# A perceiver block on one core: the 257th key's merge and the softmax division move into the cross-attention loop

## The chip, the cores and the metric

One core of one Trainium2 chip. The time is that of one execution on the device in microseconds (us); before the change it is 735.66 us, the median of 3 runs (734.97 to 736.78). The engines are TensorE (PE), VectorE (DVE), ScalarE (ACT), GpSimd (POOL) and SyncE (SP). Each runs its own instructions in program order, and they meet at semaphores. SP and ACT also issue DMAs, each from its own queue.

## What is computed

```python
x = x + xattn(layernorm(x), ctx, mask)   # 128 batches of 32 queries, 257 keys, 16 heads of 8
x = x + attn(layernorm(x))               # self-attention, 32 keys, rotary, 4 key heads
x = x + ffn(layernorm(x))                # 8 experts, one for each token
# xattn: softmax(where(mask == 0, -1e9, q k / sqrt(8))) v, times Wo, plus bo
```

The 257th key of the cross-attention is the odd one out: 256 keys fill two blocks of 128, and the last one is worked apart and merged in.

## The kernel before

**Loop.** The cross-attention takes the 128 batches in pairs: step p = 4i + r does pair p (two batches, 256 keys each), two pairs make a tile t of 128 rows of x, and 64 steps in loops over i (four steps each) make the stage. All engines go through the same steps, each with a program of its own.

**One step.** PE (`step`, L1147): the energies of pair p with the mask added (`energies`, which wait for POOL's mask `pool_m` and, once per tile, for `pool_q`), `attend` of pair p - 2, the last turn of pair p - 1, `keys` of p + 2, turn 0, `values` of p + 1, turns 1 and 2. `values` and `attend` share bank 6. DVE (L1615): three minima, `evac_out` of pair p - 2 (a copy to OC, which waits until POOL is done with that buffer, `pool_o`), the last minima, three copies of turned probabilities, the context's transpose. ACT (L665): three evacuations (`evac_k`, `evac_values`, `evac_third`), then eight exponents. POOL (`tile`, L869): for each tile the queries by head QB, two masks MZ (`masked_keys`), and `keep_own` of tile t - 3, three operations that cut the heads' own parts out of OC and put them in OT. SP (`load_pair`, L523): eight context DMAs and two mask DMAs for each pair, four pairs ahead.

**The merge.** The exponents' sums and minima of 256 keys lie in STAT. The last key's energies (`last_energies`) are taken in the last two steps of PE. After the loop, DVE takes minimum, gaps, totals and reciprocals for all tiles at once, ACT the exponents, POOL multiplies coefficients out (`coefficients`), ACT spreads them over a head's 8 columns (`spread`), PE turns them, POOL weighs the output (`weigh_out`) and forms the last key's values (`last_values`), DVE adds (`add_last`). Then PE projects (`out_project`, eight times four tiles), DVE adds the residual and takes the next layernorm's statistics. W1 is split into a high part (ACT) and a low part (POOL) at the end of that stage. Self-attention follows in a pipeline over 32 tiles, then the experts.

Of the kernel before, what the change touches and what calls it, by code (L numbers as in the profile page):

```python
# [17 lines left out]
P = 128  # L18
HD = 8
# [53 lines left out]
def perceiver_block(nc, x, ctx_in, mask, Wq, bq, Wk, bk, Wv, bv, Wo, bo,  # L73
# [18 lines left out]
    with ExitStack() as ctx:  # L92
# [55 lines left out]
        ML = sb("ML", [P, NT], I32)  # L148
        MLB = sb("MLB", [P, NT])
        VL = sb("VL", [P, P])  # L150
# [23 lines left out]

        KLT = sbc("KLT", [P, NB])
        KLB = sbc("KLB", [P, NB, 16])
        DIFF = sbc("DIFF", [P, 2, 4, NT, NG])
        MIN = sbc("MIN", [P, 4, NT, NG])
        TOTAL = sbc("TOTAL", [P, 4, NT, NG])
        COEF = sbc("COEF", [P, 2, NT, 4 * NG])  # L180
        VLT = sbc("VLT", [P, NT, P])
        OC = sbc("OC", [P, 2, BT * P])
        CX = sbc("CX", [P, 4, 2, KEYS // 32, 32])
        MK = sbc("MK", [P, 4, 2, KEYS], I32)
# [53 lines left out]
        SPREAD = TQ  # L238
        RTO = xg
        OTP = SX  # L240
        ELAST = DIFF[:, 1, :, :, :]

        CLAST = xt[:, 0, :]
        CLT = xt[:, 1, :]
        v_last = nc.dram_tensor("v_last", (NB, P), F32, kind="Internal").ap()
# [78 lines left out]
        ld_ml = sem("ld_ml")  # L324
# [7 lines left out]
        mlb_ok = sem("mlb_ok")  # L332
        st_vl = sem("st_vl")
        ld_vl = sem("ld_vl")
        pe_el = sem("pe_el")
        pe_stat = sem("pe_stat")
        m_diff = sem("m_diff")
        m_exp = sem("m_exp")
        m_inv = sem("m_inv")
        m_coef = sem("m_coef")  # L340

        act_spread = sem("act_spread")
        act_r = sem("act_r")
        pool_clv = sem("pool_clv")
        pool_t1 = sem("pool_t1")
        pe_ra = sem("pe_ra")
        pe_rb = sem("pe_rb")
        dve_otn = sem("dve_otn")
# [157 lines left out]

        small_q = [(ident, c_ident), (wv_s, Wv), (wq_s, Wq), (wo_s, Wo)]
# [9 lines left out]
        def _(sp):  # L518
# [4 lines left out]
            def load_pair(p, k, first):  # L523
# [11 lines left out]
                for e in range(2):  # L535
                    sp.dma_start(MK[:, k, e, :], mask[bass.ds(2 * p + e, 1), :, 0:KEYS]
                                 .broadcast_to([4, SQ, KEYS])).then_inc(ld_mask[k], 16)
# [3 lines left out]
            with sp.Fori(1, NP // 4) as i:  # L541
# [10 lines left out]
            sp.dma_start(ML[:, :], mask.rearrange("(i b) s k -> (b s) i k", b=BT)[:, :, KEYS],  # L552
                         allow_slow_non_contiguous=True).then_inc(ld_ml, 16)
            sp.wait_ge(st_vl, 16)
            for b in range(BT):
                sp.dma_start(VLT[b * SQ:(b + 1) * SQ, :, :],
                             v_last.rearrange("(i b a) c -> b a i c", b=BT, a=1)[b].broadcast_to([SQ, NT, P]))\
                    .then_inc(ld_vl, 16)
# [26 lines left out]
        def _(act):  # L585
# [72 lines left out]

            def evac_third(i, r):
# [22 lines left out]
            act.wait_ge(vl_ok, 1)  # L682
            act.dma_start(v_last, VL[:, :]).then_inc(st_vl, 16)
            step_range(act, step)
            evac_third(NP // 4, -1)

            act.wait_ge(m_diff, 4)
            nc.scalar.activation(DIFF[:, :, :, :, :], DIFF[:, :, :, :, :], ACT.Exp).then_inc(m_exp, 1)

            def spread(u, j):
                if u % 2 == 0:
                    act.wait_ge(m_coef, u + 1)
                wait_reuse(act, pe_ra, u - 1)
                nc.scalar.activation(SPREAD[:, j, :, :].rearrange("p i (h d) -> p (i h) d", d=HD),
                                     COEF[:, 0, 4 * u:4 * u + 4, :].rearrange("p i (h a) -> p (i h) a", a=1)
                                     .broadcast_to([P, 64, HD]), ACT.Copy).then_inc(act_spread, 1)

            def evac_inverse(u, j):
                act.wait_ge(pe_ra, u + 1)  # L700
                wait_reuse(act, pool_t1, u - 1)
                nc.scalar.activation(RTO[:, j, :], psum[6 + j][:, :], ACT.Copy).then_inc(act_r, 1)

            for u in range(NT // 4 + 1):
                if u < NT // 4:
                    spread(u, u % 2)
                if u:
                    evac_inverse(u - 1, (u - 1) % 2)

            act.wait_ge(ld_ffn, 32)
            nc.scalar.activation(W1H[:, :, :], w1_s[:, :, :], ACT.Copy).then_inc(w1_h, 1)

# [45 lines left out]
            def evac_o(t, j):  # L760
# [3 lines left out]

            act.wait_ge(n1_shift, 1)
            centre(0, 0)
            pipeline(act, [(1, evac_xv), (5, evac_probs), (-1, centre), (3, exp_scores), (5, evac_o),
                           (1, evac_last_values)], NT, 4, 6)
# [58 lines left out]
        def _(pool):  # L827
# [25 lines left out]
            def masked_keys(k):  # L853
                nc.gpsimd.tensor_scalar(MZ[:, k, :, :], MK[:, k, :, :], 0.0, None, ALU.is_equal).then_inc(pool_m, 1)  # L854
# [14 lines left out]
            def tile(i, h, first):  # L869
# [4 lines left out]
                for e in range(2):  # L874
                    masked_keys(2 * h + e)
                if not (isinstance(t, int) and t < 3):
                    keep_own(t - 3, (h + 1) % 2)

            for u in range(NT // 4):
# [6 lines left out]
                if u == 5:  # L886
                    pool.wait_ge(ld_mask[0], 32)
                    masked_keys(0)
            for k in (1, 2, 3):
                pool.wait_ge(ld_mask[k], 32)  # L890
                masked_keys(k)
                if k == 1:
                    queries_by_head(1, 1, True)
            pool.wait_ge(n0_tr, NT // 4)
# [8 lines left out]
            pool.wait_ge(klt_ok, 1)  # L903
            nc.gpsimd.tensor_tensor(
                KLB[:, :, :], KLT[:, :].rearrange("p (n a) -> p n a", a=1).broadcast_to([P, NB, 16]),
                head16[:, :].rearrange("p (a h) -> p a h", a=1).broadcast_to([P, NB, 16]), ALU.mult)\
                .then_inc(klb_ok, 1)
# [18 lines left out]
            pool.wait_ge(ld_ml, 16)  # L926
            nc.gpsimd.tensor_scalar(MLB[:, :], ML[:, :], 0.0, BIG, ALU.is_equal, ALU.mult).then_inc(mlb_ok, 1)
            for t in range(NT - 3, NT):
                keep_own(t, t % 2)

            def coefficients(c):
                cs = slice(8 * c, 8 * c + 8)
                pool.wait_ge(m_inv, c + 1)
                for w in range(2):
                    nc.gpsimd.tensor_tensor(COEF[:, w, cs, :].rearrange("p i (g k) -> p k i g", g=NG),  # L936
                                            DIFF[:, w, :, cs, :], TOTAL[:, :, cs, :], ALU.mult).then_inc(m_coef, 1)

            def last_values(u, j):
                if u % 2 == 0:  # L940
                    pool.wait_ge(m_coef, u + 2)
                wait_reuse(pool, pe_rb, u - 1)
                nc.gpsimd.tensor_tensor(SPREAD[:, 2 + j, :, :].rearrange("p i (h d) -> p (i h) d", d=HD),  # L943
# [1012 lines left out]
```

## Time and profile before

| | |
|---|---|
| median of 3 runs | 735.66 us |
| profiled execution | 738.79 us, its span 737.0 us |
| busy over the span | PE 92%, DVE 81%, ACT 68%, POOL 56% |
| mean granted clock of TensorE | 0.961 of full |

PE busy is counted from modelled ends of matmuls, so a full PE is not a PE at its peak. Idle time of an engine that does not hold the others up costs nothing. A row of a timeline begins with its start and duration in us; the square bracket at its end gives idle time of the engine before it and what ended it.

### The profile page before, as it was taken

How to read it: one execution, taken by the hardware profiler on the slowest of the kernel's cores; microseconds unless marked ns; L12 is line 12 of the kernel's file. 1: busy time of each engine (PE TensorE's matmuls, PEld its weight loads, DVE VectorE, ACT ScalarE, POOL GpSimd, SP SyncE). 2: the span in 40 equal slices, each digit the busy share in tenths (PEclk: the TensorE clock that was granted, in tenths of full speed). 3: DMA queues.
4: the chain of work that ended last, by engine and by line, in shares of the span. 5: the costliest groups of instructions: out<-in, count | busy, mean ns of one | idle time of the engine just before them, and what ended most of it. 6: DMA issues, size and time to landing. Idle time of an engine off the chain costs nothing.

```text
span 737.0 us, 29352 instructions
## 1 busy us (share of the span) xinstructions
PE 678.4 (92%) x9915; PEld 529.0 (72%) x9915; DVE 595.0 (81%) x1460; ACT 501.9 (68%) x1561; POOL 414.7 (56%) x435
## 2 busy tenths in 40 slices
PE   4999999999999999999999955999999849999994
PEld 2577777777777777777777744787777638888894
DVE  6688888888888888888888768488888857779484
ACT  3788888888888888888888634355555445545552
POOL 4576536546464564645455287467777648207375
PEclk9999999999999999999999989599999959999998
DMA  8444444444444444444448082000000020003721
GB/s 179 93 89 89 89 86 87 96 92 92 88 89 92 94 91 89 86 91 92 90 89 134 12 256 53 2 4 5 1 0 2 3 72 1 1 1 108 227 80 42
DMA packets 186527, 55.06 MB, mean 75 GB/s; under 512 B 146708, under 2 KB 184856, under 8 KB 186466
## 3 DMA queue, kind: packets, MB, share of 16 engines
q1 hardware_dynamic: 182768, 49.74, 31.8%
q0 software_dynamic: 1824, 3.96, 1.6%
q8 instruction: 40, 0.66, 0.4%
q10 hardware_dynamic: 1874, 0.54, 0.4%
q14 instruction: 21, 0.17, 0.1%
HBM read 44.51 MB, written 8.83 MB: 72 GB/s over the span
## 4 chain that ended last, share of the span: by engine, by line
PE 85%; DVE 7%; POOL 3%; issue 2%; ACT 1%; DMA 1%; POOLq 0%; ACTq 0%; DVEq 0%
PE bank L502 39%; PE energy L502 23%; PE bank L505 23%; POOL SX L951 1%; POOL TQ L943 1%; DVE stats L1534 1%; DMA X<-in_x 1%; PE energy L505 1%; DVE STAT L1592 0%; POOL COEF L936 0%; POOL out L1034 0%; DVE xn L1517 0%; DVE stats L1696 0%; DVE SX L1737 0%; DVE smx L1732 0%
## 5 line engine op out<-in xcount | busy, mean ns | idle before, releaser
L653 ACT ACTIVATE PR<-energy,STAT 128x256 f32<-128x256 f32 x512 | 235.6, 476 | 50.3 <-DVE STAT L1586 49.9
L505 PE MATMUL bank<-ident,PR 128*128 128x128 f32 x1024 | 160.2, 282 | 0.8 <-DVE PT L1612 0.8
L505 PEld LDWEIGHTS bank<-ident,PR 128*128 128x128 f32 x1024 | 112.5, 141 | 62.9 <-issue 33.6
L1612 DVE COPY PT<-bank 128x512 f32<-128x512 f32 x192 | 126.1, 684 | 11.4 <-PE bank L505 10.6
L847 POOL TENSOR_TENSOR QB<-QT,headmask 128x512 f32<-128x512 f32 x32 | 33.3, 1042 | 157.5 <-DMA MK<-in_mask_BxSxS_ik 99.1
L653 ACT ACTIVATION_READ_ACCUMULATOR PR<-energy,STAT (+1 forms) x512 | 105.5, 206 | 0.0
L854 POOL TENSOR_SCALAR MZ<-MK 128x512 bf16<-128x512 int32 x64 | 94.3, 1489 | 8.3 <-DMA MK<-in_mask_BxSxS_ik 8.3
L1592 DVE TENSOR_REDUCE STAT<-energy 128x512 f32 (+1 forms) x128 | 87.3, 682 | 0.0
L1586 DVE TENSOR_REDUCE STAT<-energy 128x256 f32 (+1 forms) x128 | 48.4, 420 | 39.3 <-PE energy L502 39.3
L502 PE MATMUL bank<-PT,VT 128*32 128x128 f32 x2048 | 69.2, 276 | 0.1
L502 PE MATMUL bank<-wv_s,CT 128*128 128x128 f32 x512 | 67.8, 275 | 0.5 <-issue 0.5
L502 PEld LDWEIGHTS bank<-PT,VT 128*32 128x32 f32 x2048 | 52.0, 109 | 21.4 <-issue 19.1
L502 PE MATMUL energy<-KS,QB 32*128 32x256 f32 x1024 | 66.1, 374 | 0.0
L502 PE MATMUL bank<-CT,wk_s 128*128 128x512 f32 x128 | 65.6, 594 | 0.0
L502 PEld LDWEIGHTS bank<-wv_s,CT 128*128 128x128 f32 x512 | 62.4, 192 | 1.0 <-issue 1.0
L752 ACT ACTIVATE SX<-SX 128x512 f32<-128x512 f32 x32 | 20.2, 631 | 52.6 <-DVE SX L1737 52.6
L502 PEld LDWEIGHTS energy<-KS,QB 32*128 32x128 f32 x1024 | 49.6, 185 | 3.5
L502 PE MATMUL energy<-w_s,TQ 128*128 128x128 f32 x384 | 48.1, 277 | 1.1 <-ACT TQ L793 0.9
L502 PEld LDWEIGHTS energy<-w_s,TQ 128*128 128x128 f32 x384 | 45.7, 192 | 3.8 <-ACT TQ L793 1.9
L987 POOL TENSOR_TENSOR SX<-SX,sinv 128x512 f32<-128x512 f32 x32 | 33.6, 1049 | 26.4 <-DVE sinv L1747 26.4
L1556 DVE STREAM_TRANSPOSE CT<-CX 128x512 f32<-128x512 f32 x64 | 44.9, 702 | 1.5 <-DMA CX<-in_ctx 1.5
L621 ACT ACTIVATE KS<-bank,bias 128x512 f32<-128x512 f32 x64 | 45.3, 709 | 0.6 <-PE bank L502 0.6
(272 smaller groups left out, 1410.2 us busy)
## 6 DMA issues: line engine op xcount, KB each, us to landing
CX<-in_ctx SPq DMA_DIRECT2D x512, 32.0 KB, 2.5
MK<-in_mask_BxSxS_ik SPq DMA_DIRECT2D x128, 128.0 KB
rows_in<-fill SPq DMA_DIRECT2D x1, 3483.0 KB, 19.6
X<-in_x SPq DMA_DIRECT2D x4, 512.0 KB, 7.4
VLT<-v_last SPq DMA_DIRECT2D x4, 512.0 KB, 9.9
PAY<-rows_in SPq DMA_DIRECT2D x2, 903.0 KB, 7.4
PAY<-X SPq DMA_DIRECT2D x1, 1280.0 KB, 6.8
w_s<-in_L_ffn_W SPq DMA_DIRECT2D x1, 1024.0 KB, 5.4
```

The source lines that it names most:

```text
L502: return nc.tensor.matmul(o, l, r, start=start, stop=stop, skip_group_check=True)
L505: return nc.tensor.transpose(o, i, ident[0:n, 0:n])
L621: nc.scalar.activation(KS[:, k % 2, :], psum[0][:, :], ACT.Identity, bias=bias[:, 1:2])\
L653: nc.scalar.activation(PR[:, b, g, :], EB[:, g, e * KEYS:(e + 1) * KEYS], ACT.Exp, bias=STAT[:, bass.ds(t, 1), b, 1, g:g + 1].rearrange("p ...
L752: nc.scalar.activation(SX[:, j, :, :], SX[:, j, :, :], ACT.Exp, scale=SCALE).then_inc(a_ex, 1)
L847: nc.gpsimd.tensor_tensor(QB[:, k, :, :, :], QT[:, bass.ds(t * P, P)].rearrange("p (b a q) -> p b a q", b=BT, a=1).broadcast_to([P, BT, 4, ...
L854: nc.gpsimd.tensor_scalar(MZ[:, k, :, :], MK[:, k, :, :], 0.0, None, ALU.is_equal).then_inc(pool_m, 1)
L987: nc.gpsimd.tensor_tensor(SX[:, j, :, :], SX[:, j, :, :], sinv[:, j, :].rearrange("p (n a) -> p n a", a=1).broadcast_to([P, 16, SQ]), ALU. ...
L1556: V.transpose(CT[:, k % 2, :], CX[:, k, :, :, :].rearrange("p e n i -> p (e n i)")).then_inc(ev_l, 1)
L1586: V.tensor_reduce(STAT[:, bass.ds(t, 1), 2 * (k % 2), 1, g:g + 1].rearrange("p a g -> p (a g)"), EB[:, g, 0:KEYS], AX_X, ALU.min).then_inc ...
L1592: V.tensor_reduce(STAT[:, bass.ds(t, 1), b:b + 2, 1, g:g + 1].rearrange("p a b g -> p (a b g)"), EB[:, g, :].rearrange("p (e k) -> p e k", ...
L1612: V.tensor_copy(PT[:, k % 2, u, :, :], psum[1 if u % 2 else 7].rearrange("p (n k) -> p n k", n=2))\
```

## The change

The 257th key's energies are taken in steps 0 and 1 (PE), turned in step 2, and kept. The division and the merge are made per group v of two tiles (four pairs) in the loop. DVE: `last_energy` in step (v, 3), `gaps`, `totals`, `coefficients` in steps 0 to 2 of iteration v + 1, each in up to three parts between and behind its copies, the last a transpose to COEFT. ACT: `gap_exponents` in step 1 of iteration v + 1; in iteration v + 2 it stores COEFT to DRAM in step 0 (`send_coefficients`), and in steps 2 and 3 it loads the third and fourth quarter back, each row to the 8 columns of its head (`spread_coefficients`, 64 KB each). SP loads the first two quarters between its pair loads. POOL weighs the output of group i - 2 at the end of its iteration i, with three operations on 256 columns, and notes the last key's mask in `masked_keys`. The two late query blocks both go to step 0. What stood in the merge stage goes, but for the two last groups; the projection reads OT. W1's split goes in eight pieces into the self-attention pipeline (`weights_high`, `weights_low`, steps 4 to 11).

```diff
@@ def send_coefficients / spread_coefficients (new; eng is SP or ACT)
+        def send_coefficients(eng, v):
+            eng.wait_ge(m_turned, v + 1)
+            eng.dma_start(coef_rows[bass.ds(v, 1), :, :].rearrange("a p c -> p (a c)"), COEFT[:, :]).then_inc(st_cf, 16)
+
+        def spread_coefficients(eng, v, groups):
+            eng.wait_ge(st_cf, 16 * v + 16)
+            tail = static(v) and v == NV - 1
+            if not tail:
+                wait_reuse(eng, pool_t1, v)
+            for g in groups:
+                eng.dma_start((COEFL if tail else COEFS)[32 * g:32 * g + 32, :, :, :].rearrange("p n w q -> p (n w q)"),
+                              coef_rows[bass.ds(v, 1), :, :].rearrange("a (h g n) c -> g h a (n c)", h=4, g=NG)[g]
+                              .broadcast_to([4, HD, 16 * SQ])).then_inc(ld_cl if tail else ld_cf, 16)
@@ SP (the mask loads take all S2 = 257 keys)
+            with sp.Fori(3, NP // 4) as i:
+                for k in range(4):
+                    load_pair(i * 4 + k, k, False)
+                    if k == 1:
+                        spread_coefficients(sp, i - 3, (0, 1))
+            spread_coefficients(sp, NV - 3, (0, 1))
...
+            for v in (NV - 2, NV - 1):
+                send_coefficients(sp, v)
+                spread_coefficients(sp, v, range(NG) if v < NV - 1 else (0, 1))
+            sp.wait_ge(ld_cl, 16 * NG)
@@ ScalarE, step(i, r), between evac_third(i, r - 1) and the exponents
+                if r == 1 and not (start and p < 4):
+                    gap_exponents(i - 1)
+                elif not (start and p < 8):
+                    if r == 0:
+                        send_coefficients(act, i - 2)
+                    else:
+                        spread_coefficients(act, i - 2, (r,))
@@ GpSimd
-            def masked_keys(k):
-                nc.gpsimd.tensor_scalar(MZ[:, k, :, :], MK[:, k, :, :], 0.0, None, ALU.is_equal).then_inc(pool_m, 1)
+            def masked_keys(p, k):
+                nc.gpsimd.tensor_scalar(FL[:, k, :], MK[:, k, :, KEYS], 0.0, None, ALU.is_equal).then_inc(pool_f, 1)
+                nc.gpsimd.tensor_scalar(MZ[:, k, :, :], MK[:, k, :, 0:KEYS], 0.0, None, ALU.is_equal)\
+                    .then_inc(pool_m, 1)
+                pool.wait_ge(pool_f, 2 * p + 1)
+                nc.gpsimd.tensor_copy(MLS[:, bass.ds(2 * p, 2)], FL[:, k, :]).then_inc(pool_f, 1)
+            def weigh_out(v):
+                if static(v) and v == NV - 1:
+                    pool.wait_ge(ld_cl, 16 * NG)
+                else:
+                    pool.wait_ge(ld_cf, 16 * NG * v + 16 * NG)
+                pool.wait_ge(pool_o, 2 * v + 2)
...
+                nc.gpsimd.tensor_tensor(out_t(2 * P * v), out_t(2 * P * v), coef[:, :, 0, :], ALU.mult).then_inc(pool_w, 1)
+                nc.gpsimd.tensor_tensor(coef[:, :, 1, :], coef[:, :, 1, :],
+                                        VLD[:, bass.ds(8 * v, 8)].rearrange("p (n a) -> p n a", a=1)
+                                        .broadcast_to([P, 8, SQ]), ALU.mult).then_inc(pool_w, 1)
+                pool.wait_ge(pool_w, 2 * v + 2)
+                nc.gpsimd.tensor_tensor(out_t(P * (2 * v + 1) - P), out_t(P * (2 * v + 1) - P), coef[:, :, 1, :], ALU.add).then_inc(pool_t1, 1)
...
             with pool.Fori(2, NT // 2) as i:
                 for k in range(2):
                     tile(i, k, False)
+                weigh_out(i - 2)
...
+            keep_own(NT - 3, (NT - 3) % 2)
+            weigh_out(NV - 2)
+            keep_own(NT - 2, (NT - 2) % 2)
+            keep_own(NT - 1, (NT - 1) % 2)
+            weigh_out(NV - 1)
@@ TensorE
+                if start and p == 0:
+                    pe.wait_ge(ev_w, 1)
+                    pe.wait_ge(n0_xt, NT // 4)
+                    queries(LATE_Q, 0)
+                    queries(LATE_Q + 1, 1)
+                elif start and p == 1:
+                    last_energies(1)
                 else:
                     attend(i, r - 2)
+                if start and p == 2:
+                    turn_energies()
...
                 if now:
                     turn(i, r, 0)
+                if start and p == 0:
+                    last_energies(0)
                 if not (start and p + 1 >= NP):
                     values(i, r + 1)
...
             def out_project(u, j):
-                pe.wait_ge(dve_otn, u + 1)
+                pe.wait_ge(pool_t1, 2 * u + 2)
...
+            pe.wait_ge(act_exp, 4 * NB)
+            out_project(0, 0)
+            step(NP // 4, 1)
+            for u in range(1, NT // 4):
+                out_project(u, u % 2)
@@ VectorE
+            def merge(i, r, part):
+                if r == 3:
+                    if part == 0:
+                        last_energy(i)
+                elif not (static(i) and i == 0):
+                    (gaps, totals, coefficients)[r](i - 1, part)
...
                     evac_turned(i, r, 0)
+                    if start and p == 0:
+                        evac_energies(slice(0, 64 * LATE_Q), 1)
+                    merge(i, r, 0)
                     evac_turned(i, r, 1)
+                    merge(i, r, 1)
                 if not (start and p + 3 >= NP):
                     turn_context(i, r + 3)
+                if not last:
+                    merge(i, r, 2)
...
-            for u in range(NT // 4 + 1):
-                if u < NT // 4:
-                    add_last(u, u % 2)
...
+            for u in range(NT // 4):
+                cross_residual(u, u % 2)
+                cross_statistics(u)
```

## Rows read from the trace of the kernel before

**Rows 1.** Busy by stretch: start:end, length; PE, PEld, DVE, ACT, POOL; PEclk, DMA, GB/s.
```profile
200.00:400.00 200.00, 200.00 (x2558) 149.46 (x2551) 175.65 (x328) 173.56 (x621) 106.89 (x116) 1.00 0.47 92
...
430.00:440.00 10.00, 7.79 (x48) 6.72 (x48) 4.61 (x10) 4.11 (x8) 9.84 (x13) 0.78 1.08 315
...
462.00:472.00 10.00, 9.50 (x129) 7.93 (x128) 3.00 (x7) 2.16 (x5) 3.53 (x4) 0.50 0.01 2
...
490.00:580.00 90.00, 88.04 (x2752) 69.67 (x2752) 78.56 (x195) 48.54 (x120) 67.31 (x74) 1.00 0.01 2
```

**Rows 2.** Timeline around one step of the loop (energies to energies).
```profile
201.47 1.04 POOL L847 TENSOR_TENSOR QB<-QT,headmask 128x512 f32<-128x512 f32 x1 [4.78 <-DMA MK<-in_mask_BxSxS_ik]
...
202.48 2.94 POOL L854 TENSOR_SCALAR MZ<-MK 128x512 bf16<-128x512 int32 x2
...
205.39 1.04 POOL L860 TENSOR_TENSOR OC<-OC,headmask 128x512 f32<-128x512 f32 x1
...
205.54 0.40 PE L502 MATMUL energy<-MZ,SEL_Q 32*128 32x512 bf16 x4
...
206.50 0.73 POOL L864 TENSOR_TENSOR OC<-OC 128x256 f32<-128x256 f32 x1
...
206.94 0.76 DVE L1586 TENSOR_REDUCE STAT<-energy 128x256 f32 x2 [0.58 <-PE energy L502]
...
207.42 0.46 POOL L866 TENSOR_TENSOR OT<-OC 128x128 f32 x1 [0.18 <-POOL OC L864]
...
208.21 0.41 DVE L1607 COPY OC<-bank 128x256 f32<-128x256 f32 x1
...
210.75 0.48 ACT L653 ACTIVATE PR<-energy,STAT 128x256 f32<-128x256 f32 x1
...
211.66 0.40 PE L502 MATMUL energy<-MZ,SEL_Q 32*128 32x512 bf16 x4
```

**Rows 3.** Timeline, last steps of the loop and what follows.
```profile
407.72 0.39 PE L502 MATMUL energy<-MZ,SEL_Q 32*128 32x512 bf16 x4
...
414.69 0.40 PE L502 MATMUL energy<-MZ,SEL_Q 32*128 32x512 bf16 x4
...
425.59 0.42 DVE L1607 COPY OC<-bank 128x256 f32<-128x256 f32 x1
```

**Rows 4.** Timeline, end of the merge stage.
```profile
453.00 4.52 POOL L966 TENSOR_TENSOR W1L<-w_s,W1H 128x2048 fp32r<-128x2048 f32 x1 [0.53 <-ACT W1H L712]
...
454.62 0.67 DVE L1691 TENSOR_TENSOR X<-X,energy 128x512 f32<-128x512 f32 x1
...
455.33 0.87 DVE L1696 BATCH_NORM_STATS2 stats<-X 128x6 f32<-128x128 f32 x4
...
457.64 0.20 DVE L1499 TENSOR_TENSOR std<-stats 128x32 f32<-128x32 f32 x1
```

**Rows 5.** Instructions of line 683, the store of v_last from ACT's queue.
```profile
DMA to landing us min/median/max: 3.8/3.8/3.8
```

**Rows 6.** Timeline, start of the loop.
```profile
27.95 0.39 PE L502 MATMUL energy<-MZ,SEL_Q 32*128 32x512 bf16 x4
...
28.06 0.37 ACTq L683 DMA_DIRECT2D v_last<-VL  x1
...
29.26 0.66 ACT L621 ACTIVATE KS<-bank,bias 128x512 f32<-128x512 f32 x1
...
31.44 1.06 PE L502 MATMUL bank<-wv_s,CT 128*128 128x128 f32 x8
...
31.76 0.68 DVE L1598 TENSOR_REDUCE STAT<-energy 128x2 f32<-128x512 f32 x1
```

**Rows 7.** Costliest groups: copies of turned probabilities; xcount, busy us, mean ns.
```profile
L1612 DVE COPY PT<-bank 128x512 f32<-128x512 f32 x192 | 126.1, 684 | 11.4 <-PE bank L505 10.6
```

**Rows 8.** Instructions of tile CX, the context loads of 32 KB.
```profile
DMA to landing us min/median/max: 1.6/2.5/3.8
```

**Rows 9.** Timeline of SP's queue in the loop.
```profile
195.09 1.31 SPq L536 DMA_DIRECT2D MK<-in_mask_BxSxS_ik  x2
```

More of the change, by code:

```diff
@@ L680, in _ @@
             evac_k(0, 1)
-            act.wait_ge(vl_ok, 1)
-            act.dma_start(v_last, VL[:, :]).then_inc(st_vl, 16)
             step_range(act, step)
             evac_third(NP // 4, -1)
[L687 to L702, printed above, removed]
-            for u in range(NT // 4 + 1):
-                if u < NT // 4:
[L706 to L712, printed above, removed]
+            gap_exponents(NV - 1)
+            spread_coefficients(act, NV - 1, (2, 3))
             act.wait_ge(lg_tr, 1)
@@ L763, in evac_o, with weights_high @@
                 nc.scalar.activation(SO[:, j, :], psum[7][:, 0:P], ACT.Copy).then_inc(a_so, 1)
+            def weights_high(t, j):
+                if static(t) and 4 <= t < 4 + E:
+                    if t == 4:
+                        act.wait_ge(ld_ffn, 32)
+                    nc.scalar.activation(W1H[:, t - 4, :], w1_s[:, t - 4, :], ACT.Copy).then_inc(w1_h, 1)
             act.wait_ge(n1_shift, 1)
@@ new lines, in totals @@
+            def totals(v, part):
+                if part == 0:
+                    dve.wait_ge(m_exp, v + 1)
+                    V.tensor_tensor(by_group(SUM[:, :]), by_group(GAP[:, 0, :]), own_stats(v, 0), ALU.mult)\
+                        .then_inc(m_own, 1)
+                elif part == 1:
+                    dve.wait_ge(m_own, 6 * v + 3)
+                    V.tensor_tensor(SUM[:, :], SUM[:, :], GAP[:, 1, :], ALU.add).then_inc(m_own, 1)
+                else:
+                    dve.wait_ge(m_own, 6 * v + 4)
+                    V.reciprocal(SUM[:, :], SUM[:, :]).then_inc(m_own, 1)
@@ new lines, in coefficients @@
+            def coefficients(v, part):
+                if part == 0:
+                    dve.wait_ge(m_own, 6 * v + 5)
+                    V.tensor_tensor(COEF[:, :, :], GAP[:, :, :],
+                                    SUM[:, :].rearrange("p (a n) -> p a n", a=1).broadcast_to([P, 2, 8 * NG]),
+                                    ALU.mult).then_inc(m_own, 1)
+                elif part == 2:
+                    dve.wait_ge(m_own, 6 * v + 6)
+                    wait_reuse(dve, st_cf, 16 * v)
+                    V.transpose(COEFT[:, :], COEF[:, :, :].rearrange("p w n -> p (w n)")).then_inc(m_turned, 1)
@@ L1622, in step @@
                     pair_minimum(i, r, 2)
-                if start and p < 2:
-                    evac_query(LATE_Q + p)
-                else:
+                if start and p == 0:
+                    evac_query(LATE_Q)
+                elif not (start and p < 2):
                     evac_out(i, r - 2)
+                if start and p == NP:
+                    for part in range(3):
+                        totals(NV - 1, part)
+                    for part in range(3):
+                        coefficients(NV - 1, part)
                 if not last:
@@ L1629, in step @@
                     second_minimum(i, r)
+                if start and p == 0:
+                    evac_query(LATE_Q + 1)
+                if start and p == 1:
+                    evac_energies(slice(64 * LATE_Q, 16 * NT), 2)
+                if start and p == 2:
+                    dve.wait_ge(pe_el, 3)
+                    V.tensor_copy(ELS[:, :, :].rearrange("p g (t b) -> p b t g", b=BT),
+                                  psum[7].rearrange("p (b t g) -> p b t g", b=BT, g=NG)).then_inc(el_ok, 1)
                 if not (start and p < 1):
```

277 lines of the change are left out of this document (103 added, 174 removed).

## Prediction

> **What bounds the kernel now.** I read the chain of waits first: it runs through TensorE, step after step, until the merge stage, and there from engine to engine. Then the busy times by stretch. Between 200 and 400 us PE is busy all 200 us, DVE 175.7, ACT 173.6, POOL 106.9 [rows 1]. So the loop is held by PE, and POOL, whose work nearly all moves are made to, looks half free. Then the timeline of one step. A step lasts 6.12 us (energies at 205.54 and 211.66) [rows 2]. DVE sat idle 0.58 us before its first minimum, and the last exponent (210.75, 0.48 and a read of some 0.2) is done about 0.25 us before the next energies: small slacks. POOL waits 4.78 us for a mask before it starts a tile [rows 2]. What is to be seen there is not the idle time but the order: POOL is one queue, and each tile's masks must pass through it before PE may begin that pair's energies. Last the stage behind the loop: energies of pair 63 at 414.69 [rows 3], last statistics ended at 456.20 (455.33 + 0.87) [rows 4], 41.5 us.
>
> **What goes: the merge stage.** In the new order, out_project(0) to (6) need no coefficient later than group 13, so DVE's residuals may follow right behind evac_out(63). Before, that copy ends at 426.01, 11.3 us after the energies of pair 63 [rows 3]. Eight times a residual (0.67) and four statistics (0.87) [rows 4] are 12.3 us, so statistics end 23.6 us after those energies, not 41.5: 17.9 less. Late next is the coefficient chain of group 15: coefficients at about +9 (DVE's three gap, three total and two coefficient operations lie between its copies), sent with 3.8 us [rows 5], spread with another 3 to 4, weigh_out 2.4, projection 1.2, residual and statistics 1.5: about 22. The two ends are close, so 14 to 18 may go; I take 17.8. Pair 62 also loses last_energies: its step took 6.97 us (407.72 to 414.69) [rows 3], 0.9 over a plain one. I take 0.9; zero is the other end, if that step is long for another reason. TensorE's granted clock was 0.50 (1.2 of 2.4 GHz) in 462 to 472 [rows 1], after the idle end of the merge. An idle end stays, so I leave that as it is; if it goes, up to 5 us more are saved in that stretch.
>
> **What is added at the start.** In step 0 values(1) waits until DVE has emptied bank 6 of the last energies. DVE's second minimum ends at 32.44 (31.76 + 0.68) [rows 6]; behind it now come the second query copy, a turned copy and the energies' copy, about 0.69 each by the 128x512 copies [rows 7] and the last smaller: 34.3. values(1) began at 31.44 [rows 6]; 2.9 later, less some 0.3 of small waits that it swallows: 2.6. Step 1: a short copy, 0.2. In step 2 the first turn waits for the 512-column copy that follows the second minimum, so it ends 4.49 (31.76 + 0.68 - 27.95) + 0.69 = 5.2 us into the step; with the turn's 0.6 behind it, values come at 5.8 where they came at 3.5 (31.44 - 27.95) [rows 6]: 2.3, less 0.5. Together 4.6; 3 to 6 as bounds. The widened key product KLB moves from a gap of POOL to one, and I cost it at nothing: what hides it is that POOL then waits for the third mask anyway; uncovered it is 1 us.
>
> **What is added in the loop, small operations.** Per four steps DVE gets nine operations on 32 or 64 columns. The nearest row has 0.20 us for 32 columns [rows 4], and they follow each other faster than that. That is at most 0.6 us in a step, as much as the 0.58 idle [rows 2]. I take 1 us over the whole loop. If the cover is gone (the full 0.2 and a wait for each, 0.4 us over the idle time per four steps), it is 6.6. ACT's gap exponents lie in the wait for the first minimum. The DMA instructions on ACT cost it nothing: the store of v_last was issued at 28.06 while an evacuation that stands ahead of it in the program began at 29.26 [rows 6], so the queue's front runs ahead of the engine. SP issues two spreads and waits for a store once per four pairs; as masks then come earlier than POOL wants them, I cost it at nothing, 1 us if its lead is used up.
>
> **What is added in the loop, the wait on POOL.** This decides. In iteration i POOL does tile(i, 0), tile(i, 1), weigh_out(i - 2). weigh_out needs all four spreads of that group, and ACT issues the fourth only in its step 4i + 3. Queued behind it on POOL is tile(i + 1, 0), whose masks PE needs for step 4i + 4, just one step later. Time counts from the energies of step 4i + 3:
> - ACT issues at +0.15: the copy ahead of it waits for the last turn of the step before, which ends there. If the queue did not run ahead it would be +1.2.
> - Landing. The trace has no such transfer. The context's 32 KB land in 1.6, 2.5 and 3.8 us (least, median, most) [rows 8]; v_last's 64 KB from ACT's queue took 3.8 [rows 5]. For masks (128 KB), the pair issued at 195.09 is what I take POOL to have got at 201.47 [rows 2, 9]; the second, issued halfway through the 1.31 us, took 5.7. I take 3.15, the mean of 2.5 and 3.8, since the spread is 64 KB on ACT's queue but is loaded like the context. 1.6 and 5.7 are kept for the range.
> - weigh_out: three operations on 256 columns at 0.73, with 0.18 before the dependent one, as in keep_own [rows 2]: 2.37.
> - QB 1.01 (201.47 to 202.48), the mask's new flag some 0.2 (0.46 for 128 columns bounds it), one mask 1.47 (half of 2.94) [rows 2], and 0.1 twice for semaphores.
>
> The sum is 0.15 + 3.15 + 2.37 + 1.01 + 0.2 + 1.47 + 0.2 = 8.55, against 6.12: PE stands 2.4 us.
>
> A second wait follows in the same step. DVE's evac_out needs keep_own(2i - 1), which stands in tile(i + 1, 0) behind both masks: 0.6 of small operations, 1.47, and keep_own's 2.49 (205.39 to 207.88) [rows 2] make it ready 4.45 us after the energies, where DVE wants it at 2.67 (208.21 - 205.54) [rows 2]. Queued behind evac_out on DVE are the last two minima, behind those the last four exponents, behind those the next energies. 1.78 less the 0.25 of slack is 1.5 us. Before, POOL ran more than a step ahead and neither wait was there.
>
> It happens where a further tile follows in the loop: i = 2 to 14, 13 times. 13 x (2.4 + 1.5) = 50.7.
>
> The Trainium skill (DMA: Bandwidth & Descriptors, section "Why a DMA increments its semaphore by 16 and not by 1") says that a transfer runs on as many of the 16 DMA engines, at most, as divide the slowest dimension of both its sides. By that the spread, with 4 on its source side, would run on 4 engines, and so would the mask, whose source is 4 copies; the mask's landing would be the nearer row. No row here shows how many engines a transfer had. The sum would then be the second rival's below.
>
> **The sum.** 4.6 + 1 + 50.7 - 17.8 - 0.9 = +37.6. The profiled execution took 738.79 (span 737.0 and 1.79 around it), 3.1 above the runs' median of 735.66; the difference carries over, so 735.66 + 37.6 = 773.
>
> **W1's two halves** move into the self-attention loop, eight pieces on ACT and POOL. POOL is busy 67.3 of 90 us there [rows 1], and the whole subtraction took 4.52 [rows 4], 0.57 a piece in steps of some 3.6. I cost that at nothing; 0 to 2 us if it delays the rotation queued behind it.
>
> **The rivals.**
> - *The wait on POOL does not bind, and the kernel is faster.* If POOL got the coefficients before it wants them, only start, small operations and tail would be left: 735.66 + 4.6 + 1 - 18.7 = 722.6. It decides at a landing of 0.7 us or less for the first wait (8.55 - 3.15 = 5.4 of fixed work in 6.12), and the least landing of the context is 1.6 [rows 8]. Halfway: landing 1.6 costs 0.9 each time, 11.7, and if DVE's late copy is also made up somewhere, the time is 734. For it speaks POOL's half-free share and its 4.78 us of waiting; against it that this idle time lies ahead of tiles whose masks were not needed yet, and that the order of the queue is fixed. 14 in 100, 3 of them halfway.
> - *The spread lands like a mask.* 5.7 instead of 3.15 makes the first wait 5.0: 13 x 6.5 = 84.5, together +71.4, 807. PE would then stand long enough for its clock to matter. Between 430 and 440 the granted clock was 0.78 after the idle front of the merge [rows 1], that is 4.4 us at half clock and 2.2 lost; 13 times 29 more, 836. For it speaks that masks are loading at that moment on the same engines; against it that a spread is half a mask, and not two at once. 15 in 100.
> - *SP is the one that is late.* It waits for the store of group i - 3 before it loads the next pairs. Per four pairs it issues for about 23 us of 24.5; with 5 us of waiting it would be 4 to 5 late. But PE is slower by 3.9 too, and the masks lead by a tile. If it does bind on top of the forecast by 1 us each time, 786. 6 in 100.
>
> **How the numbers follow.** The forecast, POOL's order stopping PE by 3 to 5 us in each iteration, has 65 in 100 and by itself 757 to 790 (landing 1.9 to 4.4). The range 750 to 806 leaves out most of the faster rival and the upper part of the mask-like one. Faster by over 0.3% (what a measurement of this kernel can tell, 2.2 us): 11 in 100. Within: 3, the halfway case. Slower: 86.
>
> **What would show it.** Right: idle time of PE before the energies of every fourth step, put down to POOL's masks (about 30 us in total); POOL waiting before weigh_out for the spread from ACT's line; DVE waiting for POOL before every fourth OC copy; four steps together 28 us in place of 24.5; the stage behind the last energies some 18 us shorter. Wrong: POOL's weigh_out starting without a wait, or steps that stay at 6.12 throughout. The size is wrong if the landing is under 1.9 or over 4.4 us.

## The result and the profile after

The changed kernel takes 810.96 us (median of 4 runs, 808.82 to 815.58) where the one before took 736.22 (median of the 4 runs beside it): ratio 1.1024, 95% interval 1.0967 to 1.108. The forecast was 773, with a range up to 806. The direction was right, the size was not.

The profiled execution has a span of 813.8 us, 76.8 over the one before. The starts of the energies divide that sum. From step 0 to step 3 it takes 8.1 us more, from step 3 to 11 nothing, from step 11 to 63 86.8 more, and from step 63 to the end 18.0 less (and 0.1 less ahead of step 0). The forecast had +4.6 for the start, +50.8 for the loop (its terms less 0.9) and -17.8 for the end. So the error is nearly all in the loop.

Windows of the kernel after (columns as in [rows 1]): the 200 us of the loop shown before, three pieces around one stop of PE, and two in the stage behind the merge.
```profile
200.00:400.00 200.00, 166.72 (x1951) 123.61 (x1950) 144.79 (x305) 135.20 (x482) 101.71 (x152) 0.91 0.36 75
...
206.00:207.00 1.00, 0.00 (x0) 0.00 (x0) 0.00 (x0) 0.00 (x0) 1.00 (x2) 1.00 0.00 0
207.00:208.00 1.00, 0.30 (x4) 0.31 (x8) 0.00 (x0) 0.00 (x0) 1.00 (x4) 0.81 0.00 0
208.00:211.00 3.00, 3.00 (x40) 2.12 (x40) 0.81 (x3) 0.15 (x1) 2.92 (x4) 0.50 0.15 42
...
543.00:548.00 5.00, 4.50 (x62) 3.70 (x63) 1.05 (x3) 0.77 (x2) 1.76 (x2) 0.50 0.99 297
548.00:553.00 5.00, 4.67 (x150) 3.75 (x145) 4.01 (x10) 2.04 (x5) 3.00 (x4) 0.90 0.03 9
```
PE was busy all 200 us before [rows 1]; now 33 of them are gone. POOL is busy for half of them, as it was (101.7 against 106.9): it is not short of time, its wait stands in the wrong place. The waits of the kernel after (engine, line, what it waited for: us, times, longest) say where:
```profile
POOL OT L898 <- DMA COEFS<-coef_rows: 209.4, 15, 15.9
...
PE energy L498 <- POOL MZ L858: 58.3, 13, 5.5
...
DVE OC L1595 <- POOL OT L873: 5.9, 6, 3.2
```
PE waits for POOL's mask 13 times, as forecast, but for 58 us, not 30. DVE's copy, forecast to wait for POOL each time too, does so five times in the loop, for 2.6 us together; the sixth, of 3.2, lies behind the loop. One of the 13 iterations, the timeline of the step that [rows 2] showed before:
```profile
196.01 1.31 SPq L547 DMA_DIRECT2D MK<-in_mask_BxSxS_ik  x2
...
196.83 0.40 PE L498 MATMUL energy<-MZ,SEL_Q 32*128 32x512 bf16 x4
...
197.13 0.63 ACTq L515 DMA_DIRECT2D COEFS<-coef_rows  x1
...
202.69 0.72 POOL L898 TENSOR_TENSOR OT<-OT,COEFS 128x256 f32 x1 [14.63 <-DMA COEFS<-coef_rows]
...
204.20 0.72 POOL L903 TENSOR_TENSOR OT<-OT,COEFS 128x256 f32 x1 [0.21 <-POOL COEFS L899]
204.88 1.04 POOL L850 TENSOR_TENSOR QB<-QT,headmask 128x512 f32<-128x512 f32 x1
...
206.07 1.49 POOL L858 TENSOR_SCALAR MZ<-MK 128x512 bf16<-128x512 int32 x1
...
207.70 0.62 PE L498 MATMUL energy<-MZ,SEL_Q 32*128 32x512 bf16 x4 [4.68 <-POOL MZ L858]
...
211.94 0.42 DVE L1595 COPY OC<-bank 128x256 f32<-128x256 f32 x1 [0.39 <-POOL OT L873]
```
Read it from the energies at 196.83, as the forecast's sum does. ACT issues at +0.30, the spread is there at +5.86, so it took 5.56 where 3.15 stood; weigh_out takes 2.19, QB 1.01, flag and mask 1.67, and the energies come 0.14 later, at +10.87. The chain is the forecast's, link by link; the landing alone is off. Over the 13 iterations the landing is 5.36 us (4.43 to 6.36), and the steps from 4i + 3 on last 10.67, 8.09, 6.35 and 6.14 us, against 6.13 before. The excess over four plain steps is 6.73 an iteration, 87.5 in all, where the sum had 3.9 and 50.7. The second step's excess (1.96) is larger than the forecast's second wait (1.5), and the clock goes with the difference. After its stop PE ran at a granted clock of 0.50, that is 1.2 of 2.4 GHz (windows above). In four of the 13 iterations, the one shown among them, the clock was back at 1.00 after 3.4 us, and the second step lasts 7.69 to 7.70, which is the forecast's; in the other nine it stayed at 0.50 for 6.8 us, and the second step lasts 7.80 to 8.59.

### The profile page after: what moved, and what is told of

Read it like the earlier page. It is cut to its first block, busy times and chain, and to the rows that moved or that the text cites. A ratio compares the mean times of both kernels' runs of the same rounds, so it can differ in the third digit from the quotient of the medians.

```text
span 813.8 us, 30118 instructions
## 1 busy us (share of the span) xinstructions
PE 698.5 (86%) x9851; PEld 540.8 (66%) x9851; DVE 611.1 (75%) x1577; ACT 497.2 (61%) x1567; POOL 443.9 (55%) x593
## 4 chain that ended last, share of the span: by engine, by line
PE 56%; POOL 11%; DVE 9%; DMA 9%; ACT 6%; issue 6%; POOLq 1%; DVEq 1%; ACTq 0%
PE bank L498 24%; PE energy L498 20%; PE bank L501 12%; DMA COEFS<-coef_rows 8%; ACT PR L667 4%; POOL MZ L858 2%; POOL QB L850 2%; POOL OT L898 1%; DVE STAT L1574 1%; POOL COEFS L899 1%; POOL SX L979 1%; POOL KB L971 1%; DVE PT L1600 1%; DVE stats L1522 1%; ACT KS L635 1%
## 5 line engine op out<-in xcount | busy, mean ns | idle before, releaser
L501 PE MATMUL bank<-ident,PR 128*128 128x128 f32 x1024 | 162.1, 287 | 3.8 <-DVE PT L1600 3.7
L501 PEld LDWEIGHTS bank<-ident,PR 128*128 128x128 f32 x1024 | 115.7, 143 | 67.8 <-issue 34.4
L898 POOL TENSOR_TENSOR OT<-OT,COEFS 128x256 f32 (+1 forms) x15 | 10.9, 727 | 209.4 <-DMA COEFS<-coef_rows 209.4
L858 POOL TENSOR_SCALAR MZ<-MK 128x512 bf16<-128x512 int32 x64 | 96.0, 1500 | 0.0
L498 PE MATMUL bank<-PT,VT 128*32 128x128 f32 x2048 | 80.0, 304 | 4.3 <-DVE PT L1600 4.3
L498 PEld LDWEIGHTS bank<-PT,VT 128*32 128x32 f32 x2048 | 59.5, 121 | 30.6 <-issue 24.5
L498 PE MATMUL energy<-MZ,SEL_Q 32*128 32x512 bf16 x256 | 27.9, 425 | 58.3 <-POOL MZ L858 58.3
L498 PE MATMUL energy<-KS,QB 32*128 32x256 f32 x1024 | 77.4, 425 | 0.0
L498 PEld LDWEIGHTS energy<-KS,QB 32*128 32x128 f32 x1024 | 57.1, 211 | 5.1
L498 PEld LDWEIGHTS energy<-MZ,SEL_Q 32*128 32x128 bf16 x256 | 6.6, 92 | 70.5 <-issue 66.8
```

What stands on the lines that cost most here:

```text
L498: return nc.tensor.matmul(o, l, r, start=start, stop=stop, skip_group_check=True)
L501: return nc.tensor.transpose(o, i, ident[0:n, 0:n])
L858: nc.gpsimd.tensor_scalar(MZ[:, k, :, :], MK[:, k, :, 0:KEYS], 0.0, None, ALU.is_equal)\
L898: nc.gpsimd.tensor_tensor(out_t(2 * P * v), out_t(2 * P * v), coef[:, :, 0, :], ALU.mult).then_inc(pool_w, 1)
```

## The experiments

**The late spread removed, four ways.** Theory T: the fourth spread's landing and the order on POOL's queue make the loss. Each of four kernels breaks one link of it.

ACT loads both its quarters in step 2:
```diff
-                    else:
-                        spread_coefficients(act, i - 2, (r,))
+                    elif r == 2:
+                        spread_coefficients(act, i - 2, (2, 3))
```

> ACT loads both its quarters in step 2, the fourth one step earlier. Theory T (the fourth spread's late landing stops POOL, whose queue holds the masks, 6.6 us in each of 13 iterations, 85 us in all): the first wait goes, a part of the second (DVE's evac_out behind keep_own) stays at about 0.9 us each time: 811 - 85 + 12 = 738. Rival S (the small operations and issues added to DVE and ACT cost it, not the landing): 805 to 811. Rival C (the spreads' traffic holds up masks and context on the DMA engines): above 770.

Measured: 741.58 us (738.12 to 748.95), 1.0051 of before (1.0014 to 1.0088). The first wait shrinks to 0.22 (step 6.35), the next step is 7.27, 1.14 over. T holds, within 4 us.

The same, but in step 1, behind `gap_exponents`:
```diff
                 if r == 1 and not (start and p < 4):
                     gap_exponents(i - 1)
...
+                    if not (start and p < 8):
+                        spread_coefficients(act, i - 2, (2, 3))
...
```

> ACT loads both its quarters in step 1, the fourth two steps earlier. T: both waits gone, 811 - 85 = 726, with steps of 6.13 us throughout. Rival S: 805 to 811. Rival C: above 770. If only the second wait mattered beside the first, the step from the run with step 2 to this one is worth about 12 us.

Measured: 739.90 (736.43 to 744.04), ratio 1.0027 (0.9998 to 1.0056), 14 us over the 726 expected. Both waits are gone (steps 6.12 and 6.15), but step 1 now lasts 6.99. Its timeline shows a cost that the forecast had put at nothing:
```profile
197.60 0.74 DVE L1573 TENSOR_REDUCE STAT<-energy 128x256 f32 x2
197.70 0.26 ACT L676 ACTIVATE GAP<-GAP 128x64 f32<-128x64 f32 x1 [0.33 <-DVE GAP L1633]
...
197.97 1.48 ACTq L515 DMA_DIRECT2D COEFS<-coef_rows  x2
...
199.69 0.47 ACT L667 ACTIVATE PR<-energy,STAT 128x256 f32<-128x256 f32 x1 [1.73 <-DVE STAT L1579]
...
200.76 0.44 PE L501 MATMUL bank<-ident,PR 128*128 128x128 f32 x2 [0.93 <-ACT PR L667]
```
The exponent at 199.69 is put down to one of DVE's minima (L1579), but it needs only the two before (L1573), and these ended at 198.34. What ended at 199.45 is ACT's own issuing. ACT's queue did not run ahead of the engine here: the gap exponents ahead of the two issues waited until 197.70, so the issues, 0.74 each, stood between them and the exponents, and PE waited 0.93.

SP loads all four quarters:
```diff
                     if k == 1:
-                        spread_coefficients(sp, i - 3, (0, 1))
+                        spread_coefficients(sp, i - 3, range(NG))
...
@@ ScalarE
-                    else:
-                        spread_coefficients(act, i - 2, (r,))
```

> SP loads all four quarters in step 1 or 2, ACT none. T: 726 as long as SP keeps up. The rival that SP is late: two more issues of some 0.65 us on 23 us in 24.5 and the wait for the store make it fall behind, masks come late: 740 to 786. S: 805 to 811 unless ACT's issues are what costs.

Measured: 754.56 (752.40 to 756.90), ratio 1.0202 (1.0150 to 1.0254). The rival's case: SP is late. Four steps take 27.00 us, and in that kernel SP's spreads follow each other after 26.8, with no long pause in its queue. Its lateness comes in by the same door: POOL waits for the spread ahead of weigh_out again, PE for the mask behind it (12 times, 9.5 us), and DVE's copy for keep_own (13 times, 19.1 us).

POOL weighs one tile later, transfers unchanged:
```diff
-            with pool.Fori(2, NT // 2) as i:
-                for k in range(2):
-                    tile(i, k, False)
-                weigh_out(i - 2)
+            with pool.Fori(3, NT // 2) as i:   # iteration 2 is peeled, group 13 follows
+                tile(i, 0, False)
+                weigh_out(i - 3)
+                tile(i, 1, False)
```

> The transfers stay as they are; POOL weighs group i - 3 between the two tiles of iteration i, so that no mask stands behind a fresh spread. T: 726, for the order on POOL is what makes the landing cost. C (traffic): stays above 770. S: 805 to 811.

Measured: 736.17 (733.71 to 740.64), ratio 0.9989 (0.9959 to 1.0019). With the same DMAs in flight and the same small operations on DVE and ACT, the order on POOL alone gives 75 us back; rivals S and C can't explain these. That is the cause shown. But it is 10 us over the 726 expected: four steps take 25.31. SP's queue in this kernel:
```profile
198.59 1.51 SPq L515 DMA_DIRECT2D COEFS<-coef_rows  x2
200.39 3.84 SPq L541 DMA_DIRECT2D CX<-in_ctx  x8
204.41 1.36 SPq L547 DMA_DIRECT2D MK<-in_mask_BxSxS_ik  x2
...
222.13 1.33 SPq L547 DMA_DIRECT2D MK<-in_mask_BxSxS_ik  x2
223.80 1.51 SPq L515 DMA_DIRECT2D COEFS<-coef_rows  x2
```
From spread to spread 25.21 us, issuing nearly without a pause. So SP holds the loop here: masks come late, keep_own after them, and DVE's copy waits for it (11.4 us, 13 times). SP has no long pause in the two kernels with ACT's early loads either (spread to spread 25.1 to 26.1 us). So what the second wait and ACT's issuing cost them stands beside a bound of SP that is nearly as long, and no run here takes the two apart.

**What the landing is made of.** Three kernels hold back only a part of the fourth quarter until step 3, the rest goes in step 2; here with two heads late:
```diff
+        CUT = [(2, 4, 0, 8), (0, 2, 0, 8)]   # heads, pairs of rows: early, late
...
+                    elif r == 2:
+                        spread_coefficients(act, i - 2, (2, 3), 0)
                     else:
-                        spread_coefficients(act, i - 2, (r,))
+                        spread_coefficients(act, i - 2, (3,), 1)
```

> The fourth quarter in two halves, two heads of four each (32 KB, 2 rows on the source's slowest side): one half in step 2, the other late in step 3. If the landing follows the bytes, half of what lies over the store's 1.5 us goes: 1.5 + 4.06 / 2 = 3.5 us from issue to weigh_out, and the first wait falls by 2 us, time some 811 - 27 = 784 or, as PE's clock then keeps up, 775. If it follows the count on the slowest side (2 here, 4 in the whole quarter), the late half takes as long as the whole: 5.5 us and 811.

> The same with the other cut: half of each row, all four heads (32 KB, 4 rows on the source's slowest side). Bytes and slowest side both say 3.5 us from issue to weigh_out; the time is then that of the forecast's own landing of 3.15, 773 plus what the start costs more (3.4): about 775 to 784. If landing is a fixed latency or the wait for other traffic: 5 us or more and 805 to 811.

> One head of four is late (16 KB, slowest side 8 for what is copied 8 times). By bytes 1.5 + 4.06 / 4 = 2.5 us from issue to weigh_out; by the slowest side (8 in place of 4, a quarter of the bytes) 2.0. A fixed latency: 5 us. Time by T at 2.5 us: first wait 1.7 us and the second 1.5, 13 x 3.2 = 42 where after had 85: about 765.

And two kernels leave the spread whole and thin SP's loads, so that they compute something else:
```diff
-                        sp.dma_start(CX[rows, k, e, :, :], ctx_in[..., 0:KEYS, rows] ...
+                        sp.dma_start(CX[rows, k, e, 0:KEYS // 32 if first else 2, :], ctx_in[..., 0:KEYS if first else 64, rows] ...
```

> Changed computation: from pair 4 on only 64 of 256 context rows of a batch are loaded, by as many DMAs as before; the rest of CX is old. Theory Q (the spread's landing, 5.3 us on the mean of 13, is its quiet 3.1 us and 2.2 us of queueing behind SP's loads on the DMA engines): with three quarters of the context's packets gone it falls to between 3.1 and 4 if the context is what it waits behind, and each iteration's loss falls by 2 us or more: 811 - 26 = 785 or less. Rival M (it waits behind the masks): 5 us and 805 to 811. Rival L (a fixed latency of what follows a store or runs on ACT's queue): 5.3 us.

```diff
-                    sp.dma_start(MK[:, k, e, :], mask[..., :] ...
+                    sp.dma_start(MK[:, k, e, 0:cols], mask[..., 0:cols] ...   # cols = S2 if first else 64
```

> Changed computation: from pair 4 on only 64 of 257 mask columns are loaded (256 B in place of 1028 B a row), by as many DMAs. Theory Q with the masks as what it waits behind: 3.1 to 4 us of landing and 785 or less. Rival (the context is what it waits behind): 5 us and 805 to 811. If each has a share, both runs land between 4 and 5.

Measured, one execution of each but the first; the landings are means over iterations 2 to 14 (least to most), taken from the timelines of ACT's queue, SP's queue and POOL; the last column is group 13, whose spread has no mask or context load beside it:

| kernel | time us | from the late issue to weigh_out | from the mask pair's issue ahead of it | group 13 |
|---|---|---|---|---|
| after | 810.96 | 5.36 (4.43 to 6.36) | 7.05 (6.28 to 7.46) | 3.09 |
| two heads late, 32 KB | 814.06 | 5.39 (4.74 to 6.47) | 6.80 (5.75 to 7.55) | 2.72 |
| half rows late, 32 KB | 808.48 | 5.10 (4.30 to 6.02) | 6.39 (4.92 to 7.00) | 2.45 |
| one head late, 16 KB | 808.41 | 5.06 (4.32 to 5.81) | 6.56 (5.04 to 7.53) | 2.41 |
| quarter of the context | 802.84 | 4.48 (3.73 to 5.45) | 6.65 (6.47 to 7.14) | 3.01 |
| quarter of the masks | 780.97 | 3.18 (2.90 to 3.59) | 4.50 (4.02 to 6.93) | 3.01 |

For the smaller pieces the landing that follows the bytes missed in all three: a quarter of the bytes lands 0.3 us sooner. What came is each text's other case, in which the bytes do not count (about 5 us or more). The piece's size and its cut hardly matter, for it waits behind the mask pair. The fourth column shows it best in the run with little context: spreads issued 1.1 us after the masks took 5.4, those issued 2.8 after took 3.9, and both were there 6.5 to 6.9 after the masks. That run met neither of its two numbers, and of the context's own share it leaves little: counted from the masks, the landing falls by 0.4. With thin masks the landing is 3.18, about that of a quiet queue. So a spread of 64 KB costs 3.1 us by itself, and the other 2.2 are the masks ahead of it, though these are on SP's queue and it is on ACT's. The Trainium skill (DMA: Bandwidth & Descriptors, section "Issuing engines are not separate DMA queues") says that transfers run on the same 16 DMA engines and interleave, whichever engine started them; these runs agree that the engines are the same.

The prediction found no row on how many of the engines a transfer had. The traces hold the packets, and these show it. In the kernel before, only masks moved between 196.3 and 198; there the share of the 16 engines (the last number but one) is 0.23, that is 3.7 engines. In the kernel after, in the step shown above, ACT's queue (q10) has no packet between its issue at 197.13 and 200.8 (first line), while the masks move; then the whole spread passes within 1 us, on 23.2% of 16, again 3.7 engines (the next two lines):
```profile
196.30:198.00 1.70, 1.70 (x13) 1.32 (x12) 1.70 (x4) 1.70 (x8) 0.39 (x1) 1.00 0.23 68
...
q1 hardware_dynamic: 950, 0.34, 37.2%
...
q1 hardware_dynamic: 538, 0.07, 43.0%
q10 hardware_dynamic: 34, 0.07, 23.2%
```
```profile
DMA packets 37, 0.07 MB, mean 61 GB/s; under 512 B 4, under 2 KB 4, under 8 KB 36
...
DMA packets 18, 0.03 MB, mean 27 GB/s; under 512 B 2, under 2 KB 2, under 8 KB 18
...
DMA packets 36, 0.03 MB, mean 27 GB/s; under 512 B 4, under 2 KB 36, under 8 KB 36
...
DMA packets 16, 0.02 MB, mean 14 GB/s; under 512 B 8, under 2 KB 8, under 8 KB 16
```
These are the counts on the source's slowest side (4 heads, 2 heads, 4 heads, and the 8 copies of the one head), by which the rule that the prediction cited counts the engines; the trace agrees with it. So mask and spread each had four engines, and as the spread stood still until the masks were all but through, these must have been the same four. The piece of one head, with eight, shows it within one transfer: issued at 195.67 behind a mask pair, half of its 16 packets pass between 197.2 and 197.7, none in the next 1 us, and the other half between 198.7 and 199.0, just after the last packet of the masks (198.5):
```profile
q10 hardware_dynamic: 8, 0.01, 4.7%
...
q10 hardware_dynamic: 8, 0.01, 7.8%
```
Half of it was not held up, but weigh_out needs all of it.

The run with thin masks is the forecast's own case, measured. Its timeline:
```profile
190.21 0.39 PE L498 MATMUL energy<-MZ,SEL_Q 32*128 32x512 bf16 x4
...
190.50 0.63 ACTq L515 DMA_DIRECT2D COEFS<-coef_rows  x1
...
193.70 0.73 POOL L899 TENSOR_TENSOR OT<-OT,COEFS 128x256 f32 x1 [12.22 <-DMA COEFS<-coef_rows]
...
198.73 0.40 PE L498 MATMUL energy<-MZ,SEL_Q 32*128 32x512 bf16 x4 [2.34 <-POOL MZ L859]
...
202.97 0.42 DVE L1596 COPY OC<-bank 128x256 f32<-128x256 f32 x1 [1.46 <-POOL OT L874]
```
PE stands 2.34 us and DVE's copy 1.46, where 2.4 and 1.5 were forecast; the steps are 8.50 and 7.71. It takes 780.97. Its start alone is 4.8 us dearer than forecast; without these it is 3 us over the 773.

**SP relieved too.** POOL's own queue loads all four quarters, one iteration later; it had over 4 us of waiting per tile [rows 2]. SP and ACT load none in the loop, and the last two groups stay as they were:
```diff
+                spread_coefficients(pool, i - 3, range(NG))
                 for k in range(2):
                     tile(i, k, False)
-                weigh_out(i - 2)
+                weigh_out(i - 3)
...
```

> POOL's own queue loads all four quarters of group i - 3 ahead of tile(i, 0) and POOL weighs that group behind tile(i, 1); SP and ACT load none in the loop. Theory SP (with POOL's order mended, what is left of the loop's loss is SP's issue time: 25.2 us in four steps with two spreads in the run with POOL's order changed, 26.7 with four): steps of 6.13 us throughout, loop 368 us, time 736 - 9 = 727. Rival (ACT's issue, or DVE's small operations cost that): 733 to 740. Rival (POOL is long in issuing, over 4 us for four): masks come late, over 740.

Measured: 730.57 (728.02 to 733.84), ratio 0.9932 (0.9911 to 0.9953), 0.7% faster than before. Steps are 6.15, 6.14, 6.13 and 6.15. Its loop window and the issuing on POOL:
```profile
200.00:400.00 200.00, 199.75 (x2551) 148.85 (x2544) 189.01 (x402) 174.47 (x625) 148.79 (x225) 1.00 0.50 101
```
```profile
220.36 2.63 POOL L516 DMA_DIRECT2D COEFS<-coef_rows  x4 [0.84 <-POOL OT L902]
```
PE is full again. Four issues cost POOL 2.63 us in four steps, inside its waits. DVE carries the merge at 189 busy us of 200 without holding PE up, so the small operations cost nothing that shows.

**The start.** In step 0 of the kernel after, PE stops inside the burst of last-key matmuls, and nothing in the profile is waited for:
```profile
32.23 1.17 PE L498 MATMUL bank<-KLB,QT 128*32 128x16 f32 x117
35.26 1.04 PE L498 MATMUL bank<-KLB,QT 128*32 128x16 f32 x75 [1.86 <-issue]
37.03 2.05 PE L498 MATMUL bank<-wv_s,CT 128*128 128x128 f32 x8 [0.73 <-issue]
```
All the kernels above that kept the order of PE's instructions stop after exactly 117 of the 192, for 1.5 to 2.5 us, but for the one with POOL's later weighing, which doesn't stop. 40 matmuls of 32 columns of weights and 16 of data were put at PE's front:
```diff
+            for _ in range(40):
+                mm(psum[4][0:32, 0:16], ident[:, 0:32], ident[:, 0:16])
             pe.wait_ge(ld_last, 16)
```

> The kernel with POOL's own loads and 40 small matmuls more at PE's very front, where PE waits for its first data. In five kernels PE stopped inside the burst of 192 last-key matmuls in step 0, after exactly 117 of them, for 1.8 to 2.5 us, and nothing in the profile was waited for. Theory I (PE's instructions come in blocks and the burst uses them up faster than they come): the place moves with the number of instructions ahead, to 117 - 40 = 77. Rival (it waits for data, LATE queries or KLB): the place stays at 117.

Measured, one execution: 734.67. The stop has moved, but not to where it was expected:
```profile
36.84 1.57 PE L499 MATMUL bank<-KLB,QT 128*32 128x16 f32 x165
40.67 0.43 PE L499 MATMUL bank<-KLB,QT 128*32 128x16 f32 x27 [2.26 <-issue]
```
165, not 77, and the loop began 4.5 us later. The place depends on what stands ahead in the program, which speaks for the supply of instructions, but simple blocks counted from the front do not give it. What the stop is stays open.

Last, the burst moved ahead of keys(2), its copy behind the second query copy:
```diff
                     queries(LATE_Q + 1, 1)
+                    last_energies(0)
...
                     evac_query(LATE_Q + 1)
+                    evac_energies(slice(0, 64 * LATE_Q), 1)
```

> The kernel with POOL's own loads; the 192 last-key matmuls of step 0 stand ahead of keys(2), and DVE copies their result right behind the second late query copy, so that values(1) waits for neither. PE's own work is then 6.0 + 1.8 us in step 0, and 7.8 with the stop inside the burst still 1.8 longer: 9.6 at most where it was 10.84. Time 730.6 - 1 to 3 = 728 to 730. Rival (the burst ahead of the keys delays ACT and DVE in steps 0 and 1 by as much): 730 to 732.

Measured: 731.33 (728.44 to 732.53), ratio 0.9915 (0.9890 to 0.9940), in the rival's range and not to be told from the kernel with POOL's own loads (0.9932). The burst runs through and step 0 lasts 8.10 us; one iteration (steps 11 and 12) loses 3.0 in return:
```profile
31.55 1.80 PE L499 MATMUL bank<-KLB,QT 128*32 128x16 f32 x192
...
36.55 0.40 PE L499 MATMUL energy<-MZ,SEL_Q 32*128 32x512 bf16 x4
```

## Why the prediction was wrong

- *The landing, the step that failed.* "I take 3.15, the mean of 2.5 and 3.8." Measured: 5.36, and the first wait with it 4.54 instead of 2.4. The value was right for a queue at rest (3.09, and 3.18 behind thin masks). The text had the other value, 5.7, and two reasons for it: "masks are loading at that moment on the same engines", and the cited rule, which gave mask and spread four engines each. Against them it set that a spread is half a mask, and its size turned out not to matter: what it waits for is the mask pair ahead of it. The row to ask was SP's queue: a mask pair is issued once a step and takes over 6 us to land [rows 2, 9], so nearly every spread has one ahead of it. A range of landings taken over many moments was used for one moment that was known.
- *The second rival.* Its price, 84.5 for the loop and 807 in all, met 87.5 and 811, by some luck: it had 5.0 and 1.5 for the two waits where 4.54 and 2.2 came, and with the clock added it said 836.
- *The clock.* Only the second rival priced it, at 2.2 us an iteration on top of both waits, if PE stands 5. PE stood 4.5, and the clock fell to 0.50 for 3.4 to 6.8 us. But the second and third steps' excess of 2.2 holds it together with the second wait of 1.5: a slow PE and DVE's late copy pass at the same time.
- *The order on POOL, the 13 times, the fixed 5.4 us behind the landing and the second wait:* right, by the deferred weighing, by the count of waits and by the run with thin masks (2.34 and 1.46). In the kernel after, the second wait is seen by itself only where the clock was soon back (steps of 7.69 to 7.70).
- *The start.* +8.1 instead of 4.6. The stop inside the burst is 1.9, and behind it, at a granted clock of 0.50 between 37 and 40 us, values took 2.05 us where it took 1.06 [rows 6] and the eight turns behind it 0.5 more. In the kernel that doesn't stop, steps 0 to 2 cost 4.2 more than before, so the copies' price of 4.6 was near.
- *The tail.* -18.0 behind the last energies, -17.8 forecast, but by luck: two errors cancel. The statistics end 27.6 us after them, not 23.6, for keep_own stands on POOL behind weigh_out(13):
```profile
512.69 0.72 POOL L898 TENSOR_TENSOR OT<-OT,COEFS 128x256 f32 x1 [12.62 <-DMA COEFS<-coef_rows]
...
518.94 0.45 POOL L873 TENSOR_TENSOR OT<-OC 128x128 f32<-128x128 f32 x1
...
519.49 0.42 DVE L1595 COPY OC<-bank 128x256 f32<-128x256 f32 x1 [3.24 <-POOL OT L873]
...
536.19 0.87 DVE L1730 BATCH_NORM_STATS2 stats<-X 128x6 f32<-128x128 f32 x4
```
  The 4 us come back in the next stage, whose clock is at 0.90 of full some 11 us after the statistics (548 to 553) and was still 0.50 there before [rows 1]. The prediction had named this gain, up to 5 us, and left it out. Counted from the statistics, the kernel is 5.1 us ahead by the fourth of the 32 tiles of self-attention, and it stays within 0.6 of that over the tiles that carry W1's pieces, so these cost next to nothing, as forecast.
- *SP, at nothing.* Right only because PE stopped: SP had time in iterations of 31 us. Once POOL's order is mended, SP's two spreads hold the loop at 25.3 in four steps, 0.8 over the 24.5 before.

## What to carry to other kernels

A transfer that somebody waits for landed here when the larger one issued shortly before it, on another queue, had landed; so look up what is in flight at its moment, and whether it is on the same DMA engines, rather than take the typical landing of a transfer of its size. An engine that is half idle but runs one queue in order is no place for a fresh wait ahead of work that another engine needs soon: put a whole iteration between the transfer's issue and its use. When one wait is taken away, the next bound may be an engine that only issues DMAs.

## What was not expected of the hardware

- A spread of 16 KB and one of 64 KB both took 5.1 to 5.4 us behind a mask pair, and 2.4 and 3.1 on a quiet queue. A mask or a spread kept some 3.7 of the 16 DMA engines busy, and a spread of eight engines had half of its packets through 1 us before the rest.
- Issuing a DMA on ACT cost the engine no idle time in the step shown (0.63 us at 197.13, with ACT busy throughout), and 0.74 us each where an instruction ahead of it had waited until 197.70.
- PE stopped 1.5 to 2.5 us in a burst of 192 short matmuls, waiting for nothing that the profile shows, at the same instruction in ten of the eleven kernels with that order of PE's instructions. The cause is open.
